# Pixel norms of a clustering convolution: squares as the moving operand in four column groups, inverted channel-major, turned by a matmul with unit columns

## The reference, cut to what matters

```python
nx = x_point / jnp.maximum(jnp.linalg.norm(x_point, axis=2, keepdims=True), 1e-12)
nc = c_point / jnp.maximum(jnp.linalg.norm(c_point, axis=2, keepdims=True), 1e-12)
sim = jax.nn.sigmoid(alpha * jnp.einsum('mlc,msc->mls', nx, nc) + beta)
max_v, max_i = sim.max(axis=2), sim.argmax(axis=2)
agg = cat_c.at[idx].add(mv[:, None] * cat_x)
disp = mv[:, None] * (agg[:, :-1] / agg[:, -1:])[idx]
out = jnp.einsum('nchw,dc->ndhw', disp, Wm) + bm[None, :, None, None]
```

## Time and profile before

| | |
|---|---|
| time, median of 3 runs | 4753.57 us (4753.42 to 4755.43) |
| the profiled execution: time / span of the trace | 4749.32 / 4747.4 us |
| TensorE busy | 4436.3 us, 93% of the span; 984 us of the millisecond from 1000 us on |
| VectorE, ScalarE, GpSimd busy | 76%, 70%, 68% |
| TensorE's share of the chain that ended last | 70% |

### The profile page before, as it was taken

One profiled execution on the slowest core, in us unless ns is written; L12 is line 12 of the kernel. 1 busy time (PEld: TensorE's weight loads), 2 busy tenths in 40 slices (PEclk: granted clock), 3 DMA queues, 4 the chain that ended last, 5 costly groups with the idle time before them and its releaser, 6 DMA issues.

```text
span 4747.4 us, 141619 instructions
## 1 busy us (share of the span) xinstructions
PE 4436.3 (93%) x51792; PEld 4259.2 (90%) x51792; DVE 3599.6 (76%) x7894; ACT 3326.7 (70%) x8843; POOL 3219.1 (68%) x3519
## 2 busy tenths in 40 slices
PE   2888999999999999999999999999999999999992
PEld 2788999999999999999999999999999999999982
DVE  5766778887887878887788878887788777777763
ACT  5766677777777777777777767777777776666652
POOL 2555666676777777777777767777777777777762
PEclk8999999999999999999999999999999999999996
DMA  5544455586877778777777767777678776666668
GB/s 182 126 100 110 113 121 129 136 189 165 186 189 186 181 169 189 184 189 178 174 189 181 190 164 182 190 186 187 162 187 191 186 167 145 155 150 156 155 153 261
DMA packets 1823073, 798.83 MB, mean 168 GB/s; under 512 B 1629216, under 2 KB 1629616, under 8 KB 1822384
## 3 DMA queue, kind: packets, MB, share of 16 engines
q1 hardware_dynamic: 1822384, 789.77, 68.7%
HBM read 395.15 MB, written 260.05 MB: 138 GB/s over the span
## 4 chain that ended last, share of the span: by engine, by line
PE 70%; POOL 13%; issue 6%; POOLq 4%; ACT 3%; DMA 2%; SPq 1%; DVE 1%; ACTq 0%; DVEq 0%
PE bank L1136 48%; PE bank L1302 8%; PE bank L1244 6%; PE bank L1289 4%; POOL xl L722 3%; PE bank L1275 3%; POOL vals L729 2%; POOL dl L736 2%; POOL vpart L676 2%; POOL fin L682 2%; DMA out<-fin 1%; DMA chunk<-x 1%; ACT xh L874 1%; ACT ysq L865 1%; POOLq L579 0%
## 5 line engine op out<-in xcount | busy, mean ns | idle before, releaser
L722 POOL TENSOR_TENSOR xl<-xr,xh 128x512 fp32r<-128x512 f32 x512 | 654.7, 1279 | 584.4 <-ACT xh L874 569.9
L729 POOL TENSOR_TENSOR vals<-vals,vpart 128x528 f32<-128x528 f32 x512 | 614.8, 1201 | 519.2 <-ACT vpart L915 519.1
L1036 DVE TENSOR_TENSOR gath<-bank,mv 128x512 f32<-128x512 f32 x503 | 347.9, 692 | 622.9 <-PE bank L1244 622.0
L1021 DVE TENSOR_REDUCE rank<-bank 128x8 f32<-128x512 f32 x1024 | 694.8, 690 | 94.4 <-PE bank L1136 81.5
L849 ACT ACTIVATE yh<-bank,bpf 128x256 fp32r<-128x256 f32 x1024 | 428.4, 469 | 364.6 <-PE bank L1136 363.7
L1136 PE MATMUL bank<-xh,wph 128*128 128x256 f32 x2048 | 583.8, 285 | 92.7 <-POOL xl L722 58.8
L1046 DVE TENSOR_TENSOR hot<-bank,rank 128x512 bf16<-128x512 f32 x1024 | 655.6, 682 | 0.0
L676 POOL TENSOR_TENSOR vpart<-vals,vpart 128x528 bf16<-128x528 f32 x512 | 611.6, 1194 | 64.6 <-ACT vpart L843 64.5
L736 POOL TENSOR_TENSOR dl<-dsq,dh 128x512 fp32r<-128x512 f32 x503 | 649.6, 1291 | 6.6 <-ACT dsq L917 6.4
L889 ACT ACTIVATE dh<-bank 128x512 fp32r<-128x512 f32 x503 | 299.8, 596 | 481.8 <-PE bank L1275 481.5
L1136 PE MATMUL bank<-ch,yh 128*128 128x256 f32 x2048 | 620.9, 303 | 0.0
(11 more groups left out here) (204 smaller groups left out, 13241.6 us busy)
## 6 DMA issues: line engine op xcount, KB each, us to landing
xr<-x SPq DMA_DIRECT2D x1024, 128.0 KB, 2.5
mixed<-xr SPq DMA_DIRECT2D x480, 256.0 KB, 2.6
chunk<-x SPq DMA_DIRECT2D x448, 256.0 KB, 3.9
fin<-mixed SPq DMA_DIRECT2D x448, 256.0 KB, 3.8
out<-fin SPq DMA_DIRECT2D x896, 128.0 KB, 3.4
xr<-x SPq DMA_DIRECT2D x64, 256.0 KB, 6.6
hot_t<-hot SPq DMA_TRANSPOSE x1024, 2.5
out<-hot_t SPq DMA_DIRECT2D x18, 512.0 KB, 6.0
```

The source lines that it names most:

```text
L722: pool.tensor_tensor(xl[:, G0 % 2], xr[:, G0 % SLOTS], xh[:, G0 % 2].bitcast(F32), ALU.subtract).then_inc(s_xl, 1)
L729: pool.tensor_tensor(vals[:, G2 % 2], vals[:, G2 % 2], vpart[:, 0], ALU.subtract).then_inc(s_r1, 1)
L1021: op = V.tensor_reduce(rank[:, t], sims[t], axis=AX.X, op=ALU.max)
L1036: V.tensor_tensor(g_out.rearrange("p (a c) -> p a c", c=CH) if J1 >= late and J1 % 2 else gath[:, :].rearrange("p (a c) -> p a c", c=CH), ...
```

## The change

The squared norms of a group are computed with the operands in swapped places. A 128x32 block of ones and zeros out of `hsum` (each head's column eight times over) is the weight, and the 128 pixels of `ysq` move. Each of the four matmuls writes another 32 partitions of the bank, which are four column groups of the array. The result has 128 partitions (2 tiles x 8 heads, each eight times) and 128 pixels. Guard, `Ln` and `Exp` now take 128 columns instead of 16 and work in place in `rnorm` in SBUF. A new fp32 matmul with `rnorm` as weights and 16 unit columns of `ident` turns the result back, pixel on partition, into `r_ps`. It stands in TensorE's list of the next step, behind the similarities and ahead of the projection. It adds onto `r_ps`, so ScalarE clears these 16 columns with a new activation in each step, and the aggregation waits for that clear, since both write bank 5. `mv` keeps 22 groups instead of 24 to make room, and a bf16 identity that nothing used is gone from the start.

```diff
-SIGS = 24
+SIGS = 22
...
-        rnorm = sb("rnorm", [P, TILES * HEADS])
-        lnn = sb("lnn", [P, TILES * HEADS])
+        rnorm = sb("rnorm", [P, P])
+        nothing = sb("nothing", [P, TILES * HEADS])
...
@@ scalar, behind the second small activation of the sigmoid of G2
+                    act.wait_ge(s_agg, upto(G2 - 2))
+                    nc.scalar.activation(r_ps[G2 % 2], nothing[:, :], ACT.Copy).then_inc(s_rz, 1)
...
@@ scalar, at the end of the step
-                    nc.scalar.activation(lnn[:, :], rnorm[:, :], ACT.Ln, scale=LN_SCALE)
+                    nc.scalar.activation(rnorm[:, :], rnorm[:, :], ACT.Ln, scale=LN_SCALE)
...
                     act.drain()
-                    act.wait_ge(s_agg, upto(G1 - 2))
-                    nc.scalar.activation(r_ps[G1 % 2], lnn[:, :], ACT.Exp, scale=-0.5, bias=lnbias).then_inc(s_rn, 1)
+                    nc.scalar.activation(rnorm[:, :], rnorm[:, :], ACT.Exp, scale=-0.5, bias=lnbias).then_inc(s_re, 1)
...
@@ vector
                     dve.wait_ge(s_n2, upto(G1))
-                    V.tensor_scalar(rnorm[:, :], n_ps[:, 0:TILES * HEADS], NORM2_MIN, None, ALU.max).then_inc(s_nc, 1)
+                    dve.wait_ge(s_rn, upto(G1 - 1))
+                    V.tensor_scalar(rnorm[:, :], n_ps[:, 0:P], NORM2_MIN, None, ALU.max).then_inc(s_nc, 1)
...
@@ tensor, behind the similarities of G2
+                    pe.wait_ge(s_re, upto(G2))
+                    pe.wait_ge(s_rz, upto(G2 - 2))
+                    mm(r_ps[G2 % 2], rnorm[:, :], ident[:, 0:P:CH // HPM], start=False, stop=True,
+                       skip_group_check=True).then_inc(s_rn, 1)
...
@@ tensor, ahead of the aggregation
-                    pe.wait_ge(s_z, upto(min(G3 + 1, NG - 1)))
+                    pe.wait_ge(s_rz, upto(min(G3 + 1, NG - 1)))
...
@@ tensor, the squared norms
-                            c = HEADS * t + HPM * m
-                            op = mm(n_ps[:, c:c + HPM], ysq[:, m, t * P:(t + 1) * P], hsum[:, :, 0], start=True,
-                                    stop=True)
+                            rows = CH * (M * t + m)
+                            op = mm(n_ps[rows:rows + CH, 0:P], hsum[:, :, :].rearrange("p a b -> p (a b)")[:, 0:P:HPM], ysq[:, m, t * P:(t + 1) * P],
+                                    start=True, stop=True)
```

More of the change, by code:

```diff
@@ L173, in cluster_block @@
         ident = sb("ident", [P, P])
-        identb = sb("identb", [P, P], BF16)
         gsum = sb("gsum", [P, P])
@@ L230, in cluster_block @@
         s_nc = sem("norms_guarded")
-        s_rn = sem("norms_inverted")
+        s_re = sem("norms_inverted")
+        s_rn = sem("norms_transposed")
+        s_rz = sem("norms_cleared")
+        s_r0 = sem("norms_cleared_at_first")
         s_z = sem("argument")
@@ L479, in _ @@
             pool.memset(ident[:, :], 0.0)
-            pool.memset(identb[:, :], 0.0)
             pool.memset(gsum[:, :], 1.0 / 8)
@@ L484, in _ @@
             pool.affine_select(out=ident[:, :], in_=ident[:, :], compare_op=ALU.not_equal, fill=1.0, base=0,
-                               pattern=[[-1, P]], channel_multiplier=1)
-            pool.affine_select(out=identb[:, :], in_=identb[:, :], compare_op=ALU.not_equal, fill=1.0, base=0,
                                pattern=[[-1, P]], channel_multiplier=1)
@@ L744, in _ @@
             act.wait_ge(s_zero, 1)
-            nc.scalar.activation(lnn[:, 0:1], s0_s, ACT.Ln, scale=0.0, bias=lnbias)
+            nc.scalar.activation(rnorm[:, 0:1], s0_s, ACT.Ln, scale=0.0, bias=lnbias)
             nc.scalar.activation(wmh[:, :, :], ws[:, :, 0:C], ACT.Copy).then_inc(s_wm, 1)
@@ L966, in _ @@
             V.memset(lnbias, LN2 * 10)
+            V.memset(nothing[:, :], 0.0)
+            for b in range(2):
+                V.memset(r_ps[b], 0.0)
+            dve.drain().then_inc(s_r0, 1)
             dve.wait_ge(s_const, 16 * 10)
@@ L1131, in _ @@
             pe.wait_ge(s_zero, 1)
+            pe.wait_ge(s_r0, 1)
             def three(out, terms):
```

## The result

The changed kernel takes 5184.51 us (median of 4 runs, 5183.08 to 5220.67) against 4753.49 us before. The ratio is 1.0925 with a 95% interval of 1.0877 to 1.0972: 9% slower, 431 us. The median itself lies 6 us inside the upper end of the range; the ratio times the earlier median gives 5193 us, 3 us outside it. One of the four runs, the one of 5220.67 us, had a mean granted clock of 0.901 where the other three had 0.971, and it is what lifts the ratio: those three lie between 5183 and 5186 us. Direction and mechanism came out as forecast, the size did not: 328 us were forecast.

The account below looks back on a forecast made before the run. TensorE's own list bounds the kernel; the change adds a wait for `Exp`. Chunk steps 310 + second chunks 31 + centres 38 + preparation 22 + chunkless steps 19 - idle 92 = 328 us, giving 5082 us, range 4975 to 5190.

Parts of the forecast that it names:

- The loop from the transposes over `dh` and `Exp` to the turning matmul: ScalarE's `Exp` gates TensorE's turning matmul, and the transposes gate the next `dh`; lateness paid in full, chance 0.76.
- From the end of `Exp` to the projection's pace: On TensorE: 0.05 us release, 0.25 us for two turning passes, 0.12 us for an uncovered weight load.
- The idle time before the turning matmul: Sign on TensorE: idle with `Exp` as releaser, about 0.8 us in an ordinary step, near 400 us in sum.
- the clear: New ScalarE write ahead of `dh`, 0.28 us at most, costed at nothing because ScalarE idles 1.02 us there.
- the norms: TensorE's 8 norm passes: 0.5 us a step instead of 0.98; sign range 0.25 to 0.6 us.
- The ordinary step with a diagonal: Step with chunk and diagonal: `Exp` already 0.22 us behind the projection's start, so the step grows by 0.84 us.
- the one without: Step with chunk but no diagonal: `Exp` 0.10 us behind the projection's start, so the step grows by 0.72 us.
- the steps without a chunk: `Exp` 0.51 us early, so 0.11 us more, 0.17 with diagonals averaged in; 114 steps, 19 us.
- a rival set apart that was in truth a part: the clock: TensorE's clock falls behind waits; some 85 late steps lose 1.7 us each, 145 us, giving 5227 us; chance 0.10.
- The sign that I had named for being wrong: The forecast is wrong if the clock in the loop drops from 1.00.
- a deduction that was too large: TensorE's existing idle time before the projection, 58.8 us for `xl` and 32.9 for the norms' guard; 92 us taken off.

## Why the prediction came out too low

**Right.** The loop from the transposes over `dh` and `Exp` to the turning matmul is the bound. Its terms in the ordinary step: `Exp` ends 3.19 us after `dh` starts (1643.09 - 1639.90), forecast 2.98 + 0.20 = 3.18. `Ln` takes 0.30 and `Exp` 0.40 us, forecast 0.30 and 0.39. From the end of `Exp` to the projection's pace (its second matmul at 1643.59 less 0.12) pass 0.38 us, forecast 0.42. The idle time before the turning matmul is 406 us, forecast near 400; `xl` is down to 18.9; `dh` still waits 1.07 us, so the clear (0.17 us) was indeed free; the norms take 0.45 us, forecast 0.5. The ordinary step with a diagonal grew by 0.94 us, forecast 0.84; the one without by 0.73, forecast 0.72; the steps without a chunk by 0.24 on average, forecast 0.17. Moving the turning matmul, with the tiles left in their new places, took away more than the whole loss. So the wait, with the clock that falls behind it, is what makes the change a loss.

**Wrong, a term that was missing: the place of the tiles.** The sum had no line for memory that moves. I used 2.85 us for 24 matmuls as if it belonged to the instructions. It belongs also to where their operands lie: 46 us in the changed kernel, of which some 28 are the matmuls themselves and the rest is the clock's; 62 us on the kernel before. The chain above has 2.95 us for the 24 matmuls of values and mixing; the chain of the kernel before has for the same two stages

```profile
1504.74 2.90 PE bank L1136 x24
```

and the projection adds its own share.

**Wrong, a rival set apart that was in truth a part: the clock.** I had it as another case, with 145 us and a chance of 0.10, and held that a wait of 1.76 us had left matmuls at full pace. That one did; behind others of 1.8 us the clock fell in the trace after. It happened 27 times more over the run, and costs 45 to 49 us by the count and the steps above. The sign that I had named for being wrong, a clock in the loop below 1.00, is there: 0.98 in the millisecond from 2200 us on. A mechanism whose bounds lay between nothing and 145 us belonged into the sum with a value between. The Trainium skill, in the section "A second HAM failure mode: psum-queue depth-cycling" of "TensorE: Matmul & The Clock Gate", tells of a kernel in which short idle stretches between groups of matmuls made the clock swing. The trace agrees in part: the long waits of the late steps cost clock, the ordinary ones of 0.8 us did not.

**Wrong, a deduction that was too large.** I took off all 92 us that TensorE had idled for `xl` and the guard. The wait for the guard is gone, but 18.9 us for `xl` stay, 13.4 of them a single wait. 73 us were saved, so the sum was 19 us too low here.

**What is left.** 328 us of the forecast, 28 for the matmuls' place, 45 to 49 for the clock and 19 for the deduction make 420 to 424 of the 431 us. Some 10 us stay open, no more than chips differ. So the wait itself was priced about right, and the miss comes from the two terms that the sum put at nothing, the place and the clock, and from the deduction. The upper end of the range, 5190 us, was passed by 3 us only with the run of 5220.67 us; that it was passed rather than just kept is chance, that the forecast was 103 us low is not.

## What to carry to other kernels

A result that another engine computes last in its step must not be put ahead of the bound engine's work without asking what covers its latency: here, with the same matmul, the change costs 9% when it stands in front of twelve others and gains 0.8% behind them, 2.1% with the tiles in their old places. Find where the waiting engine's own work starts the chain that it waits for, since this loop paid nearly every delay in full. When a change resizes small tiles, look at what lies behind them: run the old kernel once with the new memory layout before explaining a difference by instructions.

## What was not expected of the hardware

- The same fp32r matmuls of 256 columns follow each other at 0.114, 0.118 or 0.120 us depending on where their tiles lie. 64 bytes of padding made the whole kernel 1.5% slower (1.0147), 128 bytes 0.4% (1.0042).
- More work on TensorE inside a wait did not make the kernel slower, and by the one run of it faster: norms at 1.09 us instead of 0.46 gave 5164 against 5184 us, with 20 instead of 50 stretches at 1.2 GHz.
- From 690 to 4230 us of the changed kernel, the clock fell 32 times, each time behind a wait of 1.0 to 2.4 us in or next to a step with extra work, and never behind the 0.8 us of ordinary steps alone.
- Four column groups brought a factor of 2.39 for fp32 passes of 128 columns (558.1 against 233.8 us), not 4.
